# First group's score steps: low parts of eight packed pieces by TensorE, and a third raw buffer

## The reference, cut to what matters

```python
# x: (16, 128, 256); decoder layer with layer norm behind each part
x = layernorm(x + attention(x))         # gated linear attention, 16 heads of 16
x = layernorm(x + long_conv(x, ctx))    # pairs of channels, convolved along 128 tokens
x = layernorm(x + ffn(x))

# ffn: three matrices of 2048 x 256, packed as 4-bit codes with a scale for 32 values
vals = NVFP4_LUT[idx]
W = (vals.reshape(N, K // 32, 32) * scales[:, :, None]).reshape(N, K)
gate, up = xt @ Wg.T, xt @ Wu.T
out = (gelu_tanh(gate) * up) @ Wd.T
```

## Time and profile before

| | |
|---|---|
| median of three runs | 560.65 us (560.31 to 561.21) |
| the profiled execution | 560.49 us |
| its span, first to last instruction | 558.7 us |
| TensorE busy (products) | 532.1 us, 95% |
| VectorE busy | 374.2 us, 67% |
| ScalarE busy | 147.3 us, 26% |
| GpSimd busy | 124.4 us, 22% |
| chain that ended last | PE 81%, DVE 9%, issue 3%, DMA 3%, POOL 2%, ACT 1% |
| mean granted TensorE clock | 0.986 |

### The profile page before, as it was taken

How to read it: one execution, slowest core, us unless ns; L and a number is a source line. 1 busy time by engine, 2 the same in 40 slices (tenths; PEclk the granted TensorE clock), 3 DMA queues, 4 the chain that set the end, 5 groups by cost and what they waited for, 6 DMA issues and landing times.

```text
span 558.7 us, 8787 instructions
## 1 busy us (share of the span) xinstructions
PE 532.1 (95%) x3351; PEld 432.8 (77%) x3351; DVE 374.2 (67%) x782; ACT 147.3 (26%) x259; POOL 124.4 (22%) x195
## 2 busy tenths in 40 slices
PE   5999989999989999999999999999999999799993
PEld 5766777656878888766888888866888888688883
DVE  3999889977766668875455668874464777632334
ACT  3432320142442112242242111241422002223230
POOL 2100069300003444120003444120014561100001
PEclk9999899989999999999999999999999999899998
DMA  6532322121201110032001110040001100100001
GB/s 175 161 113 78 90 76 86 38 77 39 95 0 39 49 48 19 1 116 74 1 1 38 58 38 20 2 147 6 1 19 48 57 30 0 39 0 2 1 0 39
DMA packets 25258, 26.82 MB, mean 48 GB/s; under 512 B 2816, under 2 KB 22784, under 8 KB 25216
## 3 DMA queue, kind: packets, MB, share of 16 engines
q1 hardware_dynamic: 14208, 15.73, 9.5%
q10 hardware_dynamic: 10576, 8.95, 5.5%
q0 software_dynamic: 432, 1.57, 0.8%
HBM read 24.15 MB, written 2.10 MB: 47 GB/s over the span
## 4 chain that ended last, share of the span: by engine, by line
PE 81%; DVE 9%; issue 3%; DMA 3%; POOL 2%; ACT 1%; ACTq 0%; POOLq 0%; SPq 0%; DVEq 0%
PE bank L1049 17%; PE bank L1051 16%; PE bank L1050 16%; PE front_bank L1181 5%; PE front_bank L1184 4%; PE front_bank L1182 4%; PE front_bank L1118 3%; PE front_bank L1105 3%; PE front_bank L1153 3%; PE front_bank L1049 2%; PE front_bank L1050 2%; PE front_bank L1051 2%; DMA wo_sb<-in_woT 1%; PE front_bank L1129 1%; POOL ve L425 1%
## 5 line engine op out<-in xcount | busy, mean ns | idle before, releaser
L1049 PE MATMUL bank<-x2T_lo,ffn_hi 128*128 128x512 f32 x256 | 111.1, 434 | 3.5 <-DVE inter L991 2.1
L991 DVE TENSOR_TENSOR inter<-bank,inter 128x512 f32<-128x512 f32 x64 | 44.2, 690 | 90.0 <-PE bank L1051 89.7
L1051 PE MATMUL bank<-x2T_hi,ffn_hi 128*128 128x512 f32 x256 | 102.2, 399 | 0.0
L1050 PE MATMUL bank<-x2T_hi,ffn_lo 128*128 128x512 f32 x256 | 101.9, 398 | 0.0
L475 POOL TENSOR_TENSOR qbd<-qT_sb,ctxT_sb 128x256 f32<-128x256 f32 x128 | 79.0, 640 | 69.2 <-PE front_bank L1184 55.8
L425 POOL TENSOR_TENSOR ve<-ve,minus_half 128x2 f32<-128x2 f32 x24 | 17.4, 741 | 296.5 <-DVE ve L792 228.1
L649 ACT ACTIVATE inter_hi<-inter 128x512 fp32r<-128x512 f32 x64 | 40.4, 632 | 147.9 <-DVE inter L991 147.9
L1049 PE MATMUL bank<-ffn_lo,inter_hi 128*128 128x256 f32 x256 | 76.8, 300 | 1.1 <-DVE inter_lo L985 1.1
L643 ACT ACTIVATE inter<-bank 128x512 f32<-128x512 f32 x64 | 38.2, 597 | 136.0 <-PE bank L1051 135.9
L1051 PE MATMUL bank<-ffn_hi,inter_hi 128*128 128x256 f32 x256 | 72.1, 282 | 0.0
L1050 PE MATMUL bank<-ffn_hi,inter_lo 128*128 128x256 f32 x256 | 72.0, 281 | 0.0
(11 more groups left out here) (127 smaller groups left out, 779.5 us busy)
## 6 DMA issues: line engine op xcount, KB each, us to landing
toep_sb<-in_toep ACTq DMA_DIRECT2D x64, 128.0 KB, 2.1
xT_sb<-in_xT SPq DMA_DIRECT2D x4, 512.0 KB, 5.6
ctxT_sb<-in_ctxT SPq DMA_DIRECT2D x4, 512.0 KB, 4.5
x_sb<-in_x SPq DMA_DIRECT2D x4, 512.0 KB, 5.7
ctx_sb<-in_ctx SPq DMA_DIRECT2D x4, 512.0 KB, 6.6
out<-ctxT_sb POOLq DMA_DIRECT2D x3, 512.0 KB, 3.4
raw_w<-in_gate_p SPq DMA_DIRECT2D x8, 128.0 KB
raw_s<-in_gate_s SPq DMA_DIRECT2D x8, 128.0 KB
```

What stands on the lines that cost most here:

```text
L991: nc.vector.tensor_tensor(inter[:, n % 2, :], up_ps[:, :], inter[:, n % 2, :], ALU.mult).then_inc(inter_ready, 1)
L1049: nc.tensor.matmul(ps, w_hi, x_lo, start=start, stop=False, skip_group_check=True)
L1050: nc.tensor.matmul(ps, w_lo, x_hi, start=False, stop=False, skip_group_check=True)
L1051: return nc.tensor.matmul(ps, w_hi, x_hi, start=False, stop=stop, skip_group_check=True)
```

## The change

- Low parts. For the pieces q = 4 to 11 (`low_on_pe`) TensorE makes the low part, one piece in each score step of group 0, behind the scores: the identity times `weight` as an fp32 product of 512 columns into a PSUM bank, and the negated identity (fp32r) times `ffn_hi` added to it. ScalarE copies the bank to `ffn_lo`, behind its rounding of the same piece. VectorE's low part falls away for these eight, that is, behind the score steps 1 to 7 and once in the `rms` stage.
- Waits. VectorE's weight n waits there for TensorE's product of piece n-2 (`wlo_mm`) and not for its own low part. The identity product of piece q waits for its weight (`deq_ready`) and for the copy of piece q-2 (`wlo_act`), the second for the rounding (`whi_ready`). The projections of group 1 that write the same banks wait for all eight copies. `low_parts` lets those that need low parts wait for both makers.
- Fillers. One per score step instead of eight; four in the step behind the last, as before.
- Raw buffers. Three instead of two; pieces 0 to 2 are asked for at the start, and piece u when the weight of piece u-3 is done (`deq_ready` at u-2 instead of u-1).
- One new instruction of ScalarE at the start writes the negated identity.

```diff
+        FIRST_SCORE = START + 4
+        def low_on_pe(q):
+            return FIRST_SCORE <= q + 1 < FIRST_SCORE + NU_S
+        def low_parts(eng, k):
+            beside_scores = sum(low_on_pe(q) for q in range(k))
+            if k > beside_scores:
+                eng.wait_ge(wlo_ready, k - beside_scores)
+            if beside_scores:
+                eng.wait_ge(wlo_act, beside_scores)
...
-            fetch(0)
-            fetch(1)
+            for u in range(NRAW):
+                fetch(u)
             load(0)
-            for u in range(2, len(units)):
+            for u in range(NRAW, len(units)):
...
-                sp.wait_ge(deq_ready, u - 1)
+                sp.wait_ge(deq_ready, u - NRAW + 1)
                 fetch(u)
...
                     nc.scalar.activation(ffn_hi[:, m, :, c * QC:(c + 1) * QC], weight[:, n % 2], ACT.Copy)\
                         .then_inc(whi_ready, 1)
+                    if low_on_pe(n):
+                        act.wait_ge(wlo_mm, n + 2 - FIRST_SCORE)
+                        nc.scalar.activation(ffn_lo[:, m, :, c * QC:(c + 1) * QC],
+                                             low_ps[n % 2][:, :].rearrange("p (w n) -> p w n", w=2), ACT.Copy)\
+                            .then_inc(wlo_act, 1)
...
-                if 0 <= q < NU:
+                if 0 <= q < NU and not low_on_pe(q):
...
                     if n >= 2:
-                        dve.wait_ge(wlo_ready, n - 1)
+                        if low_on_pe(q):
+                            dve.wait_ge(wlo_mm, q + 2 - FIRST_SCORE)
+                        else:
+                            low_parts(dve, n - 1)
...
-                keep_busy(g, 8 if u < NU_S else 4)
+                if g == 0 and u < NU_S:
+                    low_part(FIRST_SCORE + u - 1)
+                    keep_busy(g, 1)
+                else:
+                    keep_busy(g, 4)
+
+            def low_part(q):
+                m, c = units[q]
+                pe.wait_ge(deq_ready, q + 1)
+                if q == FIRST_SCORE - 1:
+                    pe.wait_ge(minus_ready, 1)
+                if q >= FIRST_SCORE + 1:
+                    pe.wait_ge(wlo_act, q - FIRST_SCORE)
+                bank = low_ps[q % 2][:, :]
+                nc.tensor.matmul(bank, ident[:], weight[:, q % 2].rearrange("p w n -> p (w n)"),
+                                 start=True, stop=False, skip_group_check=True)
+                pe.wait_ge(whi_ready, q + 1)
+                nc.tensor.matmul(bank.rearrange("p (w n) -> p w n", w=2), minus_ident[:],
+                                 ffn_hi[:, m, :, c * QC:(c + 1) * QC], start=False, stop=True,
+                                 skip_group_check=True).then_inc(wlo_mm, 1)
```

More of the change, by code:

```diff
@@ L34 @@
 NTOEP = 4
+NRAW = 3
 NU_S = KT * NB
@@ L76, in decoder_layer @@
         ident = sb("ident", [P, P])
+        minus_ident = sb("minus_ident", [P, P], F32R)
         causal = sb("causal", [P, P])
@@ L143, in decoder_layer @@
         ffn_banks = psum[4:8]
-        skip_ps = x2T_ps = psum[4:6]
+        skip_ps = x2T_ps = low_ps = psum[4:6]
         def sems(*names):
@@ L151, in decoder_layer @@
             "ld_fold", "ld_wo", "ld_factors", "ld_small", "ld_xT", "ld_x", "ld_ctxT", "ld_ctx", "stored")
-        ld_w = sems("ld_w_even", "ld_w_odd")
+        ld_w = sems(*[f"ld_w{i}" for i in range(NRAW)])
         ld_toep = sems(*[f"ld_toep{i}" for i in range(NTOEP)])
@@ L172, in decoder_layer @@
         shifted, masked, deq_ready, wlo_ready = sems("shifted", "masked", "deq_ready", "wlo_ready")
+        minus_ready, wlo_mm, wlo_act = sems("minus_ready", "wlo_mm", "wlo_act")
         y_ready, st_ready, mv_ready, ve_ready, ln_ready = (
@@ L183, in decoder_layer @@
         rstd_ready = sems("rstd_ready1", "rstd_ready2", "rstd_ready3")
-        raw_w = sb("raw_w", [P, 2, QC], I32)
-        raw_s = sb("raw_s", [P, 2, QC])
+        raw_w = sb("raw_w", [P, NRAW, QC], I32)
+        raw_s = sb("raw_s", [P, NRAW, QC])
         code = sb("code", [P, 2, QC], I32)
@@ L369, in fetch @@
                 codes, scales = packed[m]
-                sp.dma_start(raw_w[:, u % 2, :], codes[:, c * QC:(c + 1) * QC]).then_inc(ld_w[u % 2], 16)
+                sp.dma_start(raw_w[:, u % NRAW, :], codes[:, c * QC:(c + 1) * QC]).then_inc(ld_w[u % NRAW], 16)
                 src = scales[:, c * QC:(c + 1) * QC].unsqueeze(1).broadcast_to([HT, P // HT, QC])
-                sp.dma_start(raw_s[:, u % 2, :], src).then_inc(ld_w[u % 2], 16)
-            fetch(0)
-            fetch(1)
+                sp.dma_start(raw_s[:, u % NRAW, :], src).then_inc(ld_w[u % NRAW], 16)
+            for u in range(NRAW):
+                fetch(u)
             load(0)
-            for u in range(2, len(units)):
+            for u in range(NRAW, len(units)):
                 if u == START + 4 + NU_S // 2:
@@ L521, in _ @@
             act.wait_ge(bd_ready, 1)
+            act.wait_ge(const_ready, 4)
+            nc.scalar.activation(minus_ident[:], ident[:], ACT.Copy, scale=-1.0).then_inc(minus_ready, 1)
             def unpack(step):
@@ L693, in unpack @@
                 if n < NU:
-                    dve.wait_ge(ld_w[n % 2], 32 * (n // 2 + 1))
+                    dve.wait_ge(ld_w[n % NRAW], 32 * (n // NRAW + 1))
                     if n:
@@ L699, in unpack @@
                     for w in range(2):
-                        nc.vector.tensor_scalar(code[:, w], raw_w[:, n % 2], 28 - 4 * w, 3, ALU.logical_shift_left,
+                        nc.vector.tensor_scalar(code[:, w], raw_w[:, n % NRAW], 28 - 4 * w, 3, ALU.logical_shift_left,
                                                 ALU.arith_shift_right).then_inc(shifted, 1)
                 q = n - 2
-                if 0 <= q < NU:
+                if 0 <= q < NU and not low_on_pe(q):
                     m, c = units[q]
@@ L712, in unpack @@
                     if n >= 2:
-                        dve.wait_ge(wlo_ready, n - 1)
+                        if low_on_pe(q):
+                            dve.wait_ge(wlo_mm, q + 2 - FIRST_SCORE)
+                        else:
+                            low_parts(dve, n - 1)
                     dve.wait_ge(masked, n + 1)
                     nc.vector.scalar_tensor_tensor(weight[:, n % 2], code_f16, 2.0 ** 14,
-                                                   raw_s[:, n % 2].unsqueeze(1).broadcast_to([P, 2, QC]),
+                                                   raw_s[:, n % NRAW].unsqueeze(1).broadcast_to([P, 2, QC]),
                                                    ALU.mult, ALU.mult).then_inc(deq_ready, 1)
@@ L1132, in sums @@
                 if mt == KT - 1 and ahead(g + 1):
+                    pe.wait_ge(wlo_act, NU_S)
                     for p in range(3):
@@ L1257, in weights_ready @@
                 if isinstance(g, int) and g == 0 and n % 2 == 0:
-                    pe.wait_ge(wlo_ready, 3 * (n // 2) + m)
+                    low_parts(pe, 3 * (n // 2) + m)
             def down(g, n, pair_done=None):
```

## The result

The changed kernel took 556.06 us (median of 6 executions, 554.60 to 557.76) against 560.58 us (6, 559.57 to 561.21) beside it: a ratio of 0.9922, with a 95% interval of 0.9899 to 0.9946. It is faster, as forecast, but by 4.5 us and not 2.8, and the time lies 0.5 us under the lower end of the range.

The account below looks back on a forecast made before the run. VectorE was taken to bound the score steps, TensorE's fillers being sized to it. From 560.49 us, 2.70 for the steps and 0.32 for the third buffer go, 0.20 for wo_sb returns: 557.7, or 557.8 against the median; range 556.6 to 560.4.

Parts of the forecast that it names:

- eighth low part: Behind the score steps, between sums and factors: one further low part leaves VectorE, forecast to bring nothing, the chain being TensorE's.
- VectorE's step and the circuit: Score steps: VectorE's step 2.73 us; VectorE and TensorE waiting for each other take 5.73 us per two steps, 2.87 each.
- The low bound: Score steps: the shortest step forecast, VectorE alone binding, 2.73 us.
- The end of the stage: After the last mask: last values product 1.66 us behind it, at 51.68, 2.70 us earlier than 54.38.
- The third buffer at the start: Start of the kernel: third piece fetched early gains 0.3 us, costs wo_sb 0.2 us, net 0.1 us gained.
- My first rival: Start of the kernel: wo_sb comes late by its upper bound, 1.9 us, giving 559.5 us; chance 0.10.
- The clock: Granted clock: stays at 1.00 through the score steps; half-clock stretch from about 58 to 61.6 us in the profile before.
- rival three: Score steps: clock falls to half, steps of 4.84 us, 563.7 us with three such steps, 571 with seven; chance 0.07.
- some 1.6 us: Behind the score steps: what the half-clock stretch at the last fillers and sixteen short sums costs the kernel before.
- the 556.2: Behind the score steps: forecast time in us if the half-clock stretch there vanishes, the opposite of its doubling.
- Rivals two and four: Score steps: two, half-clock stretch behind them doubles, 559.5 us, chance 0.08; four, handovers or ScalarE make steps 3.1 us, 560.3, 0.09.

## Why the prediction missed, point by point

It forecast 2.8 us saved, and 4.5 were measured. Of the 1.7 between them some 0.8, by difference, is the clock that these executions happened to have, 0.6 the third buffer and 0.45 the eighth low part (where the clock behind the steps is full), less 0.2 by which the steps gave less than forecast.

- **VectorE's step and the circuit: right in kind, a little too short.** 2.91 us a step against 2.87, alternating, as a circuit that covers two steps makes it. The circuit is 5.81 us, not 5.73 (both steps together, 3.01 + 2.80). The low bound was 2.80 and not 2.73: the weight starts 1.05 us behind the first shift here (33.15 to 34.20), and not 0.99 as in the first piece; why those differ I did not find out. Six steps of 0.04 more are the 0.2 us by which the stage gave less. Taking the filler off, or the product a step later, gave 2.80 in every step, which shows that TensorE's part of the circuit was what bound.
- **The end of the stage: right**, 1.65 against 1.66. In sum the stretch from the first mask to the sums got shorter by 2.3 to 2.5 us (26.71 and 26.55 before, 24.22 and 24.23 after), forecast 2.70.
- **The third buffer at the start: mis-sized.** "Net 0.1 us gained" was 0.7. I took the gain from one profile's 0.32 us of idle time. It is not a constant: the piece's landing doesn't follow wo_sb, so an early wo_sb gains up to 1.3 us (20.0 less 18.7) and a late one 0.4. And the 0.20 for wo_sb was not there. My first rival, with 1.9 us for it, is out.
- **The eighth low part: the step whose mechanism failed.** The prediction says that "the chain there is TensorE's, so it brings nothing". It is TensorE's in the profile that I had, because the clock is half there. At full clock it is VectorE's and the term is 0.45 us. I read which engine bound from one execution, in a stretch that I had myself marked as being at half clock.
- **The clock: right in the steps, wrong as a constant.** The clock stayed up in the steps, and rival three needs the wide products gone. But I took the half-clock stretches outside them as part of the kernel. They are not the same from one execution to the next, in either kernel, and each is worth 1.1 us on average. Behind the steps it is less than that, and not the "some 1.6 us" of the prediction: from the sums to the output product half clock costs 0.48 us in the kernel before (11.23 against 10.75) and 0.95 in the changed one (11.25 against 10.30). So the 556.2 that the prediction gives for the case that this stretch vanishes is near the measured time by luck. The profile of before (560.49 us, clock 0.986) lies at its low clock and, by their times of 560.31 to 561.21, the three runs shown do too; over 80 executions it averages 559.6. The changed kernel's six covered 0.986 to 0.993. Executions of the change at 0.986 took 557.7 us, next to the forecast 557.8, though by a saving of 3.2 and not 2.8, since the kernel before averages 560.9 there; the median of the six, 556.06, is what the forecast had no width for.
- **Rivals two and four are out**: in no profile did the half-clock stretch behind the steps double, and neither handovers nor ScalarE made a step longer than 3.02.

The account of the 3.7 us at equal clock: 2.4 from the first mask to the sums, 0.7 from the first mask's start, 0.45 behind the steps where the clock is full, 3.1 to 3.55 together. The rest, 0.2 to 0.6, is inside the scatter. Of the 4.5 us of the first comparison some 0.8 is the clock that these executions happened to have. What stays open is why the clock falls at a given gap in one execution and not in another.

## What to carry to other kernels

Before a term of a few tenths is set to nothing because "another engine binds there", look at the granted clock of that stretch: at half clock TensorE hides what it won't hide at full clock. Where one kernel's own executions spread wider than the effect looked for, compare executions of equal mean clock, and give the range of a forecast that spread. When TensorE's work is cut, count what keeps it busy: taking two products out of each step made this kernel 6 us slower, not faster.

## What the runs showed of the hardware that was not expected

- One and the same kernel, on the same data, took from 556.5 to 562.9 us, and its mean granted clock (0.984 to 0.996) accounts for most of it; what is left scatters by 0.7 us.
- With the values product and the scores (products with 32 rows or 32 columns) and one filler in each step, TensorE was busy 1.38 of 3.00 us before the fall, never idle for longer than 1.0 us at a time, and the clock fell to half and stayed there for 27 us. With two wide products more and idle for 0.2 us every other step it stayed at full.
- VectorE's two shifts took 0.40 us to the next start where the low part stood behind them, which doesn't read them (61.14 to 61.54), and 0.52 where the bit mask did, which waits for them by a semaphore (57.89 to 58.41): that wait for its own result costs 0.12 us.
